# A two-stage recommender kernel on one core: the top layers one step sooner, their transfers in halves

## The reference

```
x = layer_norm(dense @ Wd.T)                         # (512, 128)
y = layer_norm(e @ Ws.T)                             # (512, 26, 128), over 128
y = layer_norm(einsum('bne,pn->bep', y, Wsi))        # over the 32 projections
T = concat(x, y')                                    # (512, 33, 128)
Z = T @ T'                                           # (512, 33, 33)
z = layer_norm(Z[lower triangle] @ Wl.T)[:, :384]    # 528 -> 512, mask keeps 384
h = relu(concat(z, dense) @ W_top1 + b1)             # 640 -> 512
h = relu(h @ W_top2 + b2)                            # 512 -> 256
out = h @ W_top3                                     # (512, 1)
```

## Time and profile before

| | |
|---|---|
| median of 3 runs | 175.45 us (174.02 to 178.63) |
| the profiled execution's own time | 175.18 us |
| its span, first to last instruction | 173.4 us |
| busy: PE, DVE, ACT, POOL | 146.3, 130.8, 95.3, 104.9 us |
| chain that ended last: POOL, its issue gaps, PE | 59%, 19%, 15% |

### The profile page before, as it was taken

How to read it: one execution, slowest core, us unless ns; L and a number is a source line. 1 busy time by engine, 2 the same in 40 slices (tenths; PEclk the granted TensorE clock), 3 DMA queues, 4 the chain that set the end, 5 groups by cost and what they waited for, 6 DMA issues and landing times.

```text
span 173.4 us, 4663 instructions
## 1 busy us (share of the span) xinstructions
PE 146.3 (84%) x1825; PEld 109.5 (63%) x1825; DVE 130.8 (75%) x302; ACT 95.3 (55%) x239; POOL 104.9 (61%) x111
## 2 busy tenths in 40 slices
PE   0395387499988999999998997969998989999995
PEld 0193352376536455458796874849696848798994
DVE  6696836786867887979799996959999969773151
ACT  0302033788547788757665757655766866551320
POOL 3777777777777777777777777777777600020000
PEclk9999558997899999999999999999999999999999
DMA  4613665141111112311111132111112200100000
GB/s 127 233 23 89 268 204 151 23 147 26 36 23 34 23 23 58 71 25 33 26 34 23 32 77 50 30 23 27 23 34 64 59 13 2 40 20 21 0 0 0
DMA packets 6003, 9.59 MB, mean 55 GB/s; under 512 B 2303, under 2 KB 3538, under 8 KB 5854
## 3 DMA queue, kind: packets, MB, share of 16 engines
q0 software_dynamic: 3392, 3.45, 10.2%
q1 hardware_dynamic: 2232, 5.08, 9.8%
q10 hardware_dynamic: 358, 0.78, 1.3%
HBM read 8.01 MB, written 0.00 MB: 46 GB/s over the span
## 4 chain that ended last, share of the span: by engine, by line
POOL 59%; issue 19%; PE 15%; DMA 3%; DVE 2%; ACT 1%; DVEq 0%
POOL g_sb L262 59%; PE psB L375 2%; DMA g_sb<-in_table,row_id 1%; PE psW L355 1%; PE psZ L427 1%; PE psB L321 1%; DMA ids_sb<-in_ids 1%; PE psH L375 1%; PE psW L400 1%; PE psU L304 1%; PE psU L427 1%; PE psT L427 1%; PE psU L460 1%; PE psG L369 1%; PE psB L314 1%
## 5 line engine op out<-in xcount | busy, mean ns | idle before, releaser
L262 POOL DMA_INDIRECT g_sb<-in_table,row_id x104 | 103.5, 995 | 31.7 <-issue 31.4
L842 DVE TENSOR_TENSOR B<-psB,bias 128x512 f32<-128x512 f32 x31 | 20.0, 686 | 20.4 <-PE psB L321 20.3
L304 PE MATMUL psU<-wsi_x,g_sb 128*128 128x192 f32 (+4 forms) x128 | 22.5, 321 | 5.7 <-DVE g_sb L835 5.5
L304 PEld LDWEIGHTS psU<-wsi_x,g_sb 128*128 128x128 f32 x128 | 20.1, 199 | 10.9 <-DVE g_sb L835 8.8
L611 ACT ACTIVATE sqB<-B 128x512 f32<-128x512 f32 x31 | 19.0, 632 | 13.0 <-DVE B L842 13.0
L639 ACT ACTIVATE Zs<-psZ 32x264 f32<-32x264 f32 x59 | 22.4, 379 | 2.0 <-PE psZ L336 0.5
L321 PE MATMUL psB<-U,ws_g 64*128 64x512 f32 x64 | 20.0, 703 | 4.1 <-ACT U L600 4.0
L861 DVE TENSOR_TENSOR T<-B,rB 128x512 f32<-128x512 f32 x31 | 21.4, 692 | 1.1
L289 PEld LDWEIGHTS psG<-gram,sT 128*128 128x128 f32 x104 | 13.2, 195 | 13.9 <-ACT sT L587 10.9
L849 DVE TENSOR_REDUCE ssB<-sqB 128x16 f32<-128x512 f32 x32 | 21.7, 678 | 0.1
L289 PE MATMUL psG<-gram,sT 128*128 128x128 f32 x104 | 16.2, 295 | 1.4 <-ACT sT L587 1.4
(11 more groups left out here) (156 smaller groups left out, 220.9 us busy)
## 6 DMA issues: line engine op xcount, KB each, us to landing
g_sb<-in_table,row_id POOLq DMA_INDIRECT x104, 2.5
wl_sb<-in_wl SPq DMA_DIRECT2D x1, 1280.0 KB, 5.6
w_sb<-in_w SPq DMA_DIRECT2D x2, 512.0 KB, 3.4
w_sb<-in_w SPq DMA_DIRECT2D x1, 768.0 KB, 4.4
small_sb<-in_small SPq DMA_DIRECT2D x1, 615.5 KB, 4.3
dense_sb<-in_dense ACTq DMA_DIRECT2D x1, 512.0 KB, 4.8
Zt<-Zs SPq DMA_DIRECT2D x3, 80.0 KB
Zt<-Zs SPq DMA_DIRECT2D x3, 70.0 KB
```

The lines of the kernel that those rows point to most:

```text
L262: pool.indirect_dma_start(g_sb[:, k, h * DSP:(h + 1) * DSP], None, table, bass.IndirectOffsetOnAxis(row_id[:, 2 * k + h:2 * k + h + 1], 0) ...
L304: mm = pe.matmul(psU[:, (lo - US * j) * PROJ:(hi - US * j) * PROJ], g_sb[:, SLOTS * b + c, :], wsi_x[:, c, lo - s0:hi - s0, :], start=(n = ...
L842: dve.tensor_tensor(B[:, h, :].rearrange("p (s j) -> p s j", j=PROJ), psB[h][:, :].rearrange("p (s j) -> p s j", j=PROJ), bias[:, :].rearr ...
```

## The change

- The 512 KB of W_top1 that belong to `dense` are loaded third to last in SyncE's old order; now right after the small weights. `dense_part` takes four banks; parts 0 and 1 run in the prologue (half of part 0 ahead of the last transpose of unit 0), parts 2 and 3 in step 0. ScalarE's copy and its bias become two passes (`keep_hd`, then `bias_hd` in place in steps 4 to 7). `shift_part` moves to steps 1 to 3, the statistics of it to step 4.
- `LINEAR` is 5: each block's layers run one step sooner. Block 2 now uses the ordinary functions; its `layer2` alone follows `inner(15)`. The `third_` functions are gone.
- Each block's seven transfers are issued in two halves, the first when two units are kept, the second when four are. Of the second half, q = 4 and 6 are issued by ScalarE, in step j = 0 between `keep_u` and `rows_out`.
- In the steps that start a block ScalarE's `keep_z` stand partly ahead of `deviation_a` and `deviation_b`.

The diff, cut to its core:

```diff
-LINEAR = BU + 2
+LINEAR = BU + 1
-EARLY, ALL = (9, 9, 10), FLIN // P * CW
+EARLY, ALL = (9, 9, 9), FLIN // P * CW
+ACT_RELAYS = (4, 6)
+SHIFTS = {1: (0, 2), 2: (2, 4), 3: (4, CW)}
...
+        psD = [psW, psH, psW, psZ]
...
             sp.dma_start(ids_sb[:, 2 * FIRST_IDS:], ids[:, 2 * FIRST_IDS:]).then_inc(d_more, 16)
+            sp.wait_ge(d_small, 16)
+            sp.dma_start(w1_sb[:, KZ:, :], w1[:, KZ:, :]).then_inc(d_w1d, 16)
...
-            sp.wait_ge(gathered[7], 32)
-            sp.dma_start(w1_sb[:, KZ:, :], w1[:, KZ:, :]).then_inc(d_w1d, 16)
...
             for b in range(BLOCKS - 1):
-                sp.wait_ge(Z_kept, 4 * BU * (b + 1))
-                if b == 0:
-                    sp.wait_ge(fills, 5)
-                for q in range(7):
-                    relay(sp, b, q, 0, 2, d_zt[b])
+                for h in range(2):
+                    sp.wait_ge(Z_kept, 4 * (BU * b + 2 * h + 2))
+                    if b == 0 and h == 0:
+                        sp.wait_ge(fills, 5)
+                    for q in range(7):
+                        if h == 0 or q not in ACT_RELAYS:
+                            relay(sp, b, q, h, h + 1, d_zt[b])
...
             def linear(b, lo, hi):
                 if lo == 0:
-                    pe.wait_ge(d_zt[b], 7 * 16)
+                    pe.wait_ge(d_zt[b], 12 * 16)
+                    pe.wait_ge(d_zt_act, 2 * 16 * (b + 1))
...
-            def third_layer1():
...
-            def third_layer2(k_lo, k_hi):
...
             transposes(0)
             norms(0)
+            dense_part(0, 1, KD)
+            dense_part(1, 0, KD)
...
-                if late and j == 1 and t < UNITS - 1:
+                if late and j == 1:
                     linear(b, EARLY[b], ALL)
                 if t:
                     inner(t - 1)
-                if t == UNITS - 1:
-                    linear(b, EARLY[b], ALL)
                 if t == 0:
+                    dense_part(2, 0, KD)
                     x_sum()
+                    dense_part(3, 0, KD)
...
-                if 2 <= t < 2 + K1:
-                    dense_part(t - 2)
-                    shift_part(t - 2, t - 1 if t < 1 + K1 else CW)
+                if t in SHIFTS:
+                    shift_part(*SHIFTS[t])
...
             inner(UNITS - 1)
-            variance(LAST - 1)
-            third_layer1()
-            third_layer2(0, K1)
+            layer2(LAST - 1)
             last_block()
...
+            def bias_hd(f):
                 if f == 0:
+                    act.wait_ge(hd_kept, K1)
                     act.wait_ge(bz_ready, 1)
-                act.activation(hd[:, f, :], psW[:, :], ACT.Identity, bias=b1_z[:, f:f + 1]).then_inc(hd_ready, 1)
+                act.activation(hd[:, f, :], hd[:, f, :], ACT.Identity, bias=b1_z[:, f:f + 1]).then_inc(hd_ready, 1)
...
                 keep_u(t)
+                if late and j == 0:
+                    act.wait_ge(Z_kept, 4 * BU * (b + 1))
+                    for q in ACT_RELAYS:
+                        relay(act, b, q, 1, 2, d_zt_act)
                 if t + 1 < UNITS:
                     rows_out(t + 1)
-                else:
-                    third_squares(0)
...
             keep_z(UNITS - 1, 1)
-            deviation_w(LAST - 1)
             act.wait_ge(Z_kept, 4 * UNITS)
             for q in (1, 4):
                 relay(act, LAST, q, 1, 2, d_zt_act)
-            for g in range(2):
-                act.wait_ge(h1_added, LAST + g)
-                act.wait_ge(h2_done, LAST - 1)
-                act.activation(h1T[:, 2 * g * BS:2 * (g + 1) * BS], h1[:, 2 * g * BS:2 * (g + 1) * BS],
-                               ACT.Relu).then_inc(h1_ready, 1)
+            relu1(LAST - 1)
...
-            third_zT(1)
             for u, gq in ((UNITS - 2, 3), (UNITS - 1, 2), (UNITS - 1, 3)):
...
-            recip_w(LAST - 1)
-            third_scale_h1()
+            scale_h1(LAST - 1)
+            add_hd(LAST - 1)
             last_block()
```

More of the change, by code:

```diff
@@ L276, in transposes @@
                 for n, c in enumerate(range(lo, hi)):
+                    if u == 0 and c == hi - 1:
+                        dense_part(0, 0, 1)
                     pe.wait_ge(gathered[SLOTS * b + c], 32)
@@ L327, in inner @@
                     pe.wait_ge(U_ready, UNITS)
-                elif u:
+                elif u == 0:
+                    pe.wait_ge(hd_kept, K1)
+                else:
                     pe.wait_ge(Z_kept, 4 * u)
@@ L473, in last_block, with dense_part @@
                 mm.then_inc(y_done, 1)
-            def dense_part(f):
-                if f == 0:
+            def dense_part(f, k_lo, k_hi):
+                if f == 0 and k_lo == 0:
                     pe.wait_ge(d_w1d, 16)
[L478 to L481, removed]
+                if f == 2:
+                    pe.wait_ge(hd_kept, 1)
+                if f == 3:
+                    pe.wait_ge(xT_ready, 1)
+                for k in range(k_lo, k_hi):
+                    mm = pe.matmul(psD[f][:, :], w1_sb[:, KZ + k, f * P:(f + 1) * P], dense_sb[:, k, :],
                                    start=(k == 0), stop=(k == KD - 1))
-                mm.then_inc(hd_done, 1)
+                if k_hi == KD:
+                    mm.then_inc(hd_done, 1)
             def bias_part():
                 pe.wait_ge(d_w1, 16)
-                pe.wait_ge(x1_ready, 1)
+                pe.wait_ge(hd_kept, 3)
                 for f in range(K1):
                     for k in range(KZ):
-                        mm = pe.matmul(psH[:, f:f + 1], w1_sb[:, k, f * P:(f + 1) * P], bl_c[:, k:k + 1],
+                        mm = pe.matmul(psW[:, f:f + 1], w1_sb[:, k, f * P:(f + 1) * P], bl_c[:, k:k + 1],
                                        start=(k == 0), stop=(k == KZ - 1))
@@ L511, in x_sum @@
             def x_sum():
+                pe.wait_ge(hd_kept, 2)
                 pe.wait_ge(xT_ready, 1)
@@ L636, in keep_z @@
                     if b >= 2:
-                        act.wait_ge(d_zt[b - 2], 7 * 16)
+                        act.wait_ge(d_zt[b - 2], 12 * 16)
+                        act.wait_ge(d_zt_act, 2 * 16 * (b - 1))
                 to, product = z_places(u, gq)
@@ L658, in deviation_w @@
                     act.wait_ge(W_recip, b)
-                bank = psS[b] if b < LAST else psV
+                bank = psH if b < LAST else psV
                 act.activation(zsd[:, :], bank[:, 0:BS], ACT.Sqrt, bias=eps_c[:, :], scale=1.0 / FLIN).then_inc(W_sd, 1)
@@ L725, in _ @@
             deviation_a(0)
+            keep_hd(0)
+            keep_hd(1)
             def step(t):
@@ L743, in step @@
                     sum_wl(2 * t)
[L744 to L749, removed]
+                if t == 3:
+                    scale_wl(0)
+                    scale_wl(1)
+                if t == 4:
+                    scale_wl(2)
+                if t == 5:
+                    keep_m()
+                if 4 <= t < 4 + K1:
+                    bias_hd(t - 4)
                 if late and j == 3:
@@ L754, in step @@
                 enter_x(t)
+                ends = 0 < t < UNITS - 1 and t % BU == 0
+                if ends:
+                    keep_z(t - 1, 0)
                 if t + 1 < UNITS:
                     deviation_a(t + 1)
-                if late and j == 1 and t < UNITS - 1:
+                if t == 0:
+                    keep_hd(2)
+                if late and j == 1:
                     squares_w(b)
                 if 0 < t < UNITS - 1:
-                    keep_z(t - 1, 0)
+                    keep_z(t - 1, 1 if ends else 0)
                 deviation_b(t, 0)
@@ L764, in step @@
                     deviation_b(t, 1)
-                    third_squares(1)
                     keep_z(t - 1, 1)
                     keep_z(t - 1, 2)
+                elif ends:
+                    keep_z(t - 1, 2)
+                    keep_z(t - 1, 3)
+                    deviation_b(t, 1)
                 elif t:
@@ L776, in step @@
                     keep_x_sum()
+                    keep_hd(3)
                     sum_wl(0)
@@ L1080, in step @@
                                       ALU.mult, ALU.add).then_inc(wl_scaled, 1)
-                if 1 <= t < 1 + KZ:
-                    k = t - 1
+                if t in (1, 2, 5):
+                    k = min(t - 1, KZ - 1)
                     if k == 0:
```

71 lines of the change are left out of this document (17 added, 54 removed).

## The result

| | before | after |
|---|---|---|
| median (4 runs each) | 175.39 us | 177.64 us |
| ratio, 95% interval | | 1.0175 [1.0111, 1.0239] |
| profiled execution, its span | 175.18, 173.4 us | 177.25, 175.4 us |

The change makes the kernel slower, here by 1.1 to 2.4%, and by 0.5 to 1.8% when it was run again (`changed_again`). 175.8 was forecast; the time lies inside the range (173.7 to 178.0), but the forecast was "no change that could be measured".

A forecast was written before the change was run, and what follows sets the result against it. GpSimd's gathers were taken to pace the steady part, so time is the last gather landing plus a tail of some 34 us. Against 175.18: 0.2 + 1.03 - 0.64 = +0.6, 175.8 us, range 173.7 to 178.0.

The forecast's parts named there:

- What the tail loses: Last inner products to last block's linear: only layer 2 remains of block 2's leftover, 5.54 instead of 6.18 us, -0.64.
- Steady part: Up to the last gather: runs at the pace of GpSimd's gathers, which wait for nobody; the change leaves that so.
- the cost of 0: Dense part moved to prologue and step 0: covered, since TensorE has until step 8 to catch up; costed at 0.
- Step 13: Block 2's linear waits for second-half transfers, ScalarE's issues delay sT; unit 15's transposes end slightly later, +0.2 us.
- the old wait of 0.83: TensorE's wait for unit 15's gathered rows, expected to hide most lateness of step 13; without it 0.9 to 1.5 shows.
- My own sign: Mark of a right forecast: last transpose of unit 15 within 0.2 us or so of its gathered rows.
- Rival C: Second half of transfers lands late in step 13, making the linear wait: 177.6, up to 179.4 us; chance 0.18.
- Steps 14 and 15: From unit 15's transposes to the end of the last inner products: +1.03 us, of which step 14 is 0.8.
- Step 14: Linear products, inner products and variance stand between norms and mixing of unit 15: 6.5 instead of 5.70 us, +0.8.
- Step 15: Layer 1 of block 2 replaces ten linear products, 2.8 instead of 2.5 us; last inner products then take 1.50.
- Rival B: Step 14's added work fits behind the scaling chain and costs nothing, only the tail moves: 173.5 us; chance 0.12.
- Rival A: ScalarE's transfer issues cost nothing that counts: sT on time in step 13, tail -1.18, 175.0 us; chance 0.15.

The follow-up runs named there:

- changed_again: The changed kernel itself, run again beside other experiments on one chip: 176.99 us, ratio 1.0114 to the kernel before.
- fill: The changed kernel plus twelve idle products between the last inner products and block 2's layer 2: 175.29 us, ratio 1.0021 to the kernel before.
- dense_only: The kernel before with only the dense part moved, layers, transfers and block 2 as before: 174.07 us, ratio 0.9948.
- fill_short_var: As fill, but block 2's variance in step 14 is one product instead of four: 174.91 us, ratio 0.9976 to the kernel before.
- relays_pool: The changed kernel with the last block's two ScalarE transfers on GpSimd: 176.25 us, ratio 1.0118 to the kernel before.
- split_tail: The changed kernel with block 2's variance, layer 1 and layer 2 spread over step 15 and the tail, one last-block transfer on ScalarE: 173.95 us, ratio 0.998.
- split_tail_one: As split_tail, with one transfer instead of two on ScalarE in steps 5, 9 and 13: 173.19 us, ratio 0.994 to the kernel before.
- relays_sp: The changed kernel with all seven second-half transfers on SyncE in steps 5, 9 and 13: 178.07 us, ratio 1.0119 to the kernel before.

## Why the prediction was wrong

**What failed: "What the tail loses".** -0.64 was forecast, +0.74 measured. Every term up to layer 2 held: Zs kept 0.92 after the inner products, the issues 0.04 later (0.21 forecast), 1.66 for them (1.73), relu 0.63 and layer 2 started 3.41 after the inner products (3.49). The mis-sized term is the last, "layer 2 2.05", which became 3.51. I took it from a row in which TensorE had worked without a break, and put it behind a gap of 3.5 us that my own sum made: once variance and layer 1 are gone, TensorE has nothing to do until relu. Behind that gap its clock was halved. `fill` shows the cause by putting work into the gap and changing nothing else: the clock stays at 1.00, layer 2 takes 2.05, and the linear starts 5.29 after the inner products, 0.89 sooner than before the change, where I had forecast 0.64.

**Steady part: right for GpSimd.** Its row is unchanged and the dense part cost nothing; `dense_only` even gained 0.5%, which the cost of 0 did not hold.

**Step 13: +0.23 for +0.2, by luck in this pair of traces.** The issues stood where they were put, and sT was copied at 133.54, the late end of what I allowed (133.0 to 133.6), because U came at 131.90 instead of 131.27. Step 12 did get lighter, as I counted on: from unit 12's mixing to unit 13's it is 6.98, against 7.49 before. But unit 12's mixing itself came 0.99 late, at 123.50 instead of 122.51. Its rows came 0.39 later, and step 11 behind them took 7.36 instead of 6.76, because TensorE's clock fell there (last section). From there to its end TensorE waits for no rows any more, so the old wait of 0.83, which I counted on to hide what is late, was not there. My own sign, the transposes within 0.2 or so of their rows, is not met: they end 0.56 later behind the last gather's issue than before. That 0.23 stands in the table comes from gathers that were 0.33 sooner.

Up to step 13 six of the kernels profiled after the change do the same. In us, the last transpose of step 11 to unit 12's mixing (starts), and the issue of the last gather to the end of unit 15's transposes:

| | clock in step 11 | step 11 | behind the last gather |
|---|---|---|---|
| before (another list in these steps) | 1.00 | 6.76 | 2.85 |
| the changed kernel | 0.50 | 7.36 | 3.41 |
| `changed_again` | 0.50 | 7.43 | 3.55 |
| `fill` | 0.50 | 7.36 | 3.38 |
| `fill_short_var` | 0.50 | 7.39 | 3.48 |
| `relays_pool` | 1.00 | 6.11 | 3.09 |
| `split_tail` | 1.00 | 6.21 | 2.92 |

So step 13 by itself costs 0.07 to 0.24, about what I forecast. In `split_tail` the two issues delay nothing, since sT waits for the transposes and these wait for rows. TensorE's and ScalarE's timelines there:

```profile
130.74 0.33 PE L283 MATMUL psT<-small_sb,g_sb 128*128 128x128 f32 x1 [0.83 <-DMA g_sb<-in_table,row_id]
...
131.44 0.49 ACT L599 ACTIVATE sT<-psT 128x384 f32<-128x384 f32 x1 [1.06 <-PE psT L283]
```

A slow step 11 goes with 0.29 to 0.63 more, a term that my sum does not have. No run changes that clock alone, so its price is read from executions that also differ in their gathers.

The fifth SyncE transfer, issued at 133.83, landed in time for a linear at 136.48. Rival C, a late second half, did not come about, but only just: in `changed_again` the linear waits 0.19 for a transfer, and with SyncE alone 1.48.

**Steps 14 and 15: right in sum (+1.11 for +1.03), not in parts.** Step 14 cost 1.12 where 0.8 was forecast: besides the heavier list (`fill_short_var`), projection now waits 0.36 for U, a wait that lay inside the wait for rows before. Step 15 cost -0.01 where +0.23 was forecast; the inner products behind layer 1 took 1.17, not 1.50. That the sum fits is in part luck: 0.32 too little in one step, 0.24 too much in the other. Rival B, step 14 free, is refuted.

**Rival A**, issues that cost ScalarE nothing that counts: refuted in step 13 (sT late by 1.04; not late without issues on ScalarE, nor in `split_tail`, where the rows came last), nearly right in the tail, where they cost 0.28. The Trainium skill, "DMA: Bandwidth & Descriptors", section "Issuing engines are not separate DMA queues", calls the initiating time usually small beside the transfer; here two issues of 0.83 and 0.72 stand beside a landing of at most 2.65 (133.83 to 136.48).

The rival that was missing is the one that happened: the tail gets shorter in work and longer in time, because the work removed had kept TensorE's clock up. None of A to C holds this case.

## What to carry to other kernels

Work taken from the stretch ahead of the last dependent matmuls may have been holding the clock: look at what TensorE does in the gap that an edit opens, and don't cost the matmuls behind it by a row from a busy stretch. Rather than removing such work, spread it so that it fills the gap (`split_tail`). An issue on a compute engine's queue was nearly free where it lay beside that engine's running pass (sT 0.24 late), and cost its length where a second one followed (1.04). And two profiles are to be compared from a mark that both share, here the last gather, before a difference of some tenths is believed.

## What the runs showed of the hardware

A halved clock behind gaps this short was not expected. Behind gaps of 0.53 to 0.95 us (`fill`, `split_tail`, `split_tail_one`) layer 2 ran at full clock; behind 3.14, 3.41 and 3.47 us (`relays_pool`, the changed kernel, `relays_sp`) it did not. Shorter gaps in the steady part of the changed kernel also went ahead of it: a wait of 2.73 in step 5, where it cost the end nothing, as TensorE waited for rows again in steps 8 to 11, and one of 1.86 in step 11, behind which eight norm halves took 2.07, against 1.16 behind a wait of 1.36 in the same step before the change. Behind this second one TensorE waits for rows no more, so it did reach the transposes of unit 15 (table above). The first line is from TensorE's timeline before, the others, and the windows of step 11, are from after the change:

```profile
117.06 1.16 PE L289 MATMUL psG<-gram,sT 128*128 128x128 f32 x8
```

```profile
62.58 2.45 PE L309 MATMUL psU<-wsi_x,g_sb 128*128 128x128 f32 x8 [2.73 <-DVE g_sb L829]
...
116.14 0.33 PE L283 MATMUL psT<-small_sb,g_sb 128*128 128x128 f32 x1 [1.86 <-DMA g_sb<-in_table,row_id]
...
117.63 2.07 PE L294 MATMUL psG<-gram,sT 128*128 128x128 f32 x8
...
123.50 1.25 PE L309 MATMUL psU<-wsi_x,g_sb 128*128 128x160 f32 x8
```

```profile
116.00:117.00 1.00, 0.86 (x5) 0.44 (x5) 0.00 (x0) 0.50 (x1) 0.94 (x1) 1.00 0.27 60
117.00:118.00 1.00, 1.00 (x6) 0.38 (x2) 0.28 (x1) 0.10 (x1) 0.72 (x1) 0.61 0.25 64
118.00:119.00 1.00, 1.00 (x6) 1.00 (x6) 1.00 (x2) 0.55 (x1) 0.69 (x2) 0.50 0.20 42
```

In five of the ten traces the clock fell to 0.50 in step 11 (the changed kernel, `changed_again`, `fill`, `fill_short_var`, `dense_only`), and in five it stayed at 1.00. The length of one wait does not tell the two apart: `split_tail` kept 1.00 behind a wait of 1.61 (until 115.17), while `fill` fell to 0.50 behind one of 1.42 (until 116.49) with another 0.49 just ahead of it.

The clock fell only after TensorE had started again, and stayed at 0.50 with PE busy all the time: a slow stretch is found in the column of the granted clock, not in that of the busy time. The Trainium skill, "TensorE: Matmul & The Clock Gate", section "What's actually happening", says that the throttled state is the default and that activity releases the throttle. `fill` agrees as to the activity: with twelve products in the gap the clock stayed at 1.00 behind them. That the throttled state is the default no trace here shows: the column reads 1.00 in the first 6 us too, before the first matmul.

Gathers that take 1.0 to 1.46 us instead of 0.94 at GpSimd come and go from execution to execution; their cause stays open, as does that of the gain in `dense_only`.
